# Attribute products of the edge MLP moved into the dense stage, stored sorted, and both gathers made to add to them

## What is computed

```
h = relu(layernorm(x))
x = x + rgcn(h)            # layer 0: two relational convolutions
h = relu(layernorm(x))
x = x + gcn(h)             # layer 1
h = relu(layernorm(x))
edge_feat = concat([h[src], h[dst], edge_attr])      # 512 + 512 + 64
messages = mish(mish(edge_feat @ W1 + b1) @ W2 + b2) # layer 2
agg = segment_sum(messages, dst)
u = mish(concat([h, agg]) @ W3 + b3)
x = x + layernorm(h + u @ W4 + b4) * gamma + beta
# layer 3: relu(concat(h[src], h[dst]) @ W.T + b), summed by src
```

## Time and profile before

| | |
|---|---|
| runs | 1164.44, 1168.77, 1169.74 us, median 1168.77 us |
| profiled execution | 1167.43 us, of which the span of the trace is 1165.6 us |
| busy in the span | PE 1082.5 us (93%), DVE 856.0 (73%), ACT 557.9 (48%), POOL 498.8 (43%) |

### The profile page before, as it was taken

How to read it: one execution, slowest core, us unless ns; L and a number is a source line. 1 busy time by engine, 2 the same in 40 slices (tenths; PEclk the granted TensorE clock), 3 DMA queues, 4 the chain that set the end, 5 groups by cost and what they waited for, 6 DMA issues and landing times. The chain is left out here.

```text
span 1165.6 us, 15308 instructions
## 1 busy us (share of the span) xinstructions
PE 1082.5 (93%) x4358; PEld 588.0 (50%) x4358; DVE 856.0 (73%) x2016; ACT 557.9 (48%) x978; POOL 498.8 (43%) x434
## 2 busy tenths in 40 slices
PE   3779888899999988999999999999999989999997
PEld 1133223344557453755555555555555547446664
DVE  5997667769755153787887887887887856848997
ACT  0221321311332311577777777777777734115564
POOL 0000112243333430768876666666666200027773
PEclk9788989999999999899999999999999999999999
DMA  7996997657111005685554444444444020026665
GB/s 281 366 361 229 362 379 272 229 186 248 63 50 46 13 14 193 143 251 112 115 105 99 97 96 99 96 97 98 97 97 76 2 74 3 9 84 202 210 211 160
DMA packets 60183, 172.65 MB, mean 148 GB/s; under 512 B 12646, under 2 KB 13190, under 8 KB 52553
## 3 DMA queue, kind: packets, MB, share of 16 engines
q0 software_dynamic: 31536, 72.01, 26.3%
q1 hardware_dynamic: 28568, 99.66, 23.2%
HBM read 159.65 MB, written 11.98 MB: 147 GB/s over the span
## 5 line engine op out<-in xcount | busy, mean ns | idle before, releaser
L1630 PE MATMUL PS<-wide,hidT 128*128 128x512 f32 x672 | 302.1, 592 | 0.0
L689 POOL DMA_INDIRECT rec_scratch<-rec_src,slot_row x84 | 99.0, 1179 | 262.5 <-DMA rec_scratch<-rec_src,slot_row 211.9
L1630 PEld LDWEIGHTS PS<-wide,hidT 128*128 128x128 f32 x672 | 128.6, 191 | 122.8 <-issue 120.5
L1566 ACT ACTIVATE wide<-PS 128x512 f32<-128x512 f32 x168 | 100.3, 597 | 100.5 <-PE PS L1616 64.2
L1453 POOL DMA_INDIRECT pair_sum<-table_j,counts_rec x84 | 136.1, 1620 | 27.6 <-issue 25.3
L1758 POOL DMA_INDIRECT u_space<-table_j,wide x87 | 83.0, 955 | 111.8 <-DMA table_j<-agg_space 84.9
L1445 POOL DMA_INDIRECT pair_sum<-table_i,counts_rec x84 | 89.3, 1063 | 97.1 <-PE PS L1616 59.7
L1571 ACT ACTIVATE wide<-wide,two 128x512 f32<-128x512 f32 x168 | 120.9, 719 | 6.2 <-DVE wide L1504 6.2
L1504 DVE SCALAR_TENSOR_TENSOR wide<-wide 128x512 f32<-128x512 f32 x168 | 116.3, 692 | 5.8
L1576 ACT ACTIVATE wide<-wide 128x512 f32<-128x512 f32 x168 | 105.8, 630 | 5.3
L1462 POOL DMA_INDIRECT rec_scratch<-rec_src,slot_row x84 | 87.5, 1041 | 41.1 <-issue 21.6
(11 more groups left out here) (321 smaller groups left out, 1849.2 us busy)
## 6 DMA issues: line engine op xcount, KB each, us to landing
pieces<-basis_rows SPq DMA_DIRECT2D x56, 1024.0 KB, 7.3
ring<-basis_low SPq DMA_DIRECT2D x30, 256.0 KB, 6.2
w_scratch<-pieces SPq DMA_DIRECT2D x112, 32.0 KB
counts_rec<-rec_scratch SPq DMA_DIRECT2D x1, 2856.0 KB, 9.5
rec_scratch<-rec_src,slot_row POOLq DMA_INDIRECT x168, 2.2
root<-L_gnn_root SPq DMA_DIRECT2D x2, 1024.0 KB, 6.2
rows_in<-in_rows_in SPq DMA_DIRECT2D x2, 1024.0 KB, 15.5
w_rel<-w_scratch SPq DMA_DIRECT2D x1, 2048.0 KB, 11.1
```

The source lines that it names most:

```text
L689: nc.gpsimd.indirect_dma_start(out=rec3_dram, out_offset=bass.IndirectOffsetOnAxis(ap=slot_row[:, 1, t:t + 1], axis=0), in_=rec, in_offset ...
L1566: nc.scalar.activation(grow[l][:, t % 2, :], PS[:, bank, :], ACT.Exp).then_inc(sem(f"exp{l}"), 1)
L1630: m = nc.tensor.matmul(o, hidT[:, t % 2, k * P:(k + 1) * P], w2[:, k, :], start=False, stop=(k == KT - 1), skip_group_check=True)
```

## The change

The attribute products no longer belong to the edge loop. In the dense stage the attributes come in already turned (`attr_T`, 21 slabs of 4 tiles, doubled over the partitions: the upper 64 rows hold the same values), loaded on ScalarE's queue. ScalarE rounds a slab to a short float (float32r), VectorE replaces the second 64 rows by the remainder, and the weights are split in two likewise. TensorE then makes 128 edges x 512 outputs in two short-float passes of 128x512 (`attr_rows`), ScalarE copies them out of PSUM (`keep_attr`), and GpSimd scatters the 2 KB rows to their sorted places in HBM (`scatter_attr`). The counts of products at each place are constants: 35 in `gathered_first`, 20 after the Y1 products, 15 in the root rows, 10 in `gathered`, 4 in `both`.

In the edge stage SyncE loads the finished rows of tile t into `pair_sum`, and both gathers add to them. `pre` is four transposes. The record that GpSimd sorts is now 8 bytes, and its 84 scatters run with three in flight, before the attribute scatters, and start without waiting for layer 3's records. `is_dst3` has six buffers instead of two. The last pair numbers are read ahead of the tail.

```diff
+REC = 2
+SLAB = 4
+SLABS = ET // SLAB
+        attr_dram = dram("attr_scratch", (P * ET, D))
+            ATTR_RING, REC_RING = 6, 3
+            attr_out = lambda t: slabs[:, 4 + t % ATTR_RING, :] if t % ATTR_RING < 4 else late_f[:, 7 * P + (t % ATTR_RING - 4) * D:7 * P + (t % ATTR_RING - 3) * D]
+            FIRST_ATTR = ((0, 0, 0, 2, 2), (2, 1, 2, 1, 1), (2, 1, 2, 1, 2), (2, 1, 2, 1, 2), (2, 1, 2, 1, 2))
+            Y1_ATTR, ROOT_ATTR, GATHER_ATTR, BOTH_ATTR = 2, 3, 2, 1
@@ TensorE, dense stage @@
+                def attr_rows(number):
+                    for _ in range(number):
+                        t = next(turned_attr)
+                        pe.wait_ge(sem("attr_lo"), t // SLAB + 1)
+                        bank = turn(("A", t), alone)
+                        own = attr_split[:, t // SLAB % 2, t % SLAB * P:(t % SLAB + 1) * P]
+                        nc.tensor.matmul(PS[:, bank, :], own, w_attr_hi[:], start=True, stop=False)
+                        nc.tensor.matmul(PS[:, bank, :], own, w_attr_lo[:], start=False, stop=True).then_inc(sem("side_mm"), 1)
@@ GpSimd, dense stage @@
-                def scatter(t, rec):
-                    if t:
-                        pool.wait_ge(sem("sorted1"), 16 * t)
+                def scatter(t):
+                    if t >= REC_RING:
+                        pool.wait_ge(sem(f"sorted1_{t % REC_RING}"), 16 * (t // REC_RING))
+                def scatter_attr(t):
+                    if t >= 3:
+                        pool.wait_ge(sem(f"attr_out{(t - 3) % ATTR_RING}"), 16 * ((t - 3) // ATTR_RING) + 16)
+                    pool.wait_ge(sem("side_ev"), side["A", t] + 1)
+                    nc.gpsimd.indirect_dma_start(
+                        out=attr_dram, out_offset=bass.IndirectOffsetOnAxis(ap=slot_row[:, 1, t:t + 1], axis=0),
+                        in_=attr_out(t), in_offset=None).then_inc(sem(f"attr_out{t % ATTR_RING}"), 16)
-                pool.wait_ge(sem("rec_set"), 2)
+                pool.wait_ge(sem("slot_row1"), 1)
+                for t in range(ET):
+                    scatter(t)
+                for t in range(ET):
+                    scatter_attr(t)
@@ VectorE, dense stage @@
+                def attr_low(j):
+                    dve.wait_ge(sem("attr_hi"), j + 1)
+                    low = attr_split[ED:P, j % 2, :]
+                    nc.vector.tensor_tensor(low, attr_in[ED:P, j % 2, :], low.bitcast(F32), ALU.subtract).then_inc(sem("attr_lo"), 1)
@@ ScalarE, dense stage @@
+                def keep_attr(number):
+                    for _ in range(number):
+                        t = next(kept_attr)
+                        j = t // SLAB
+                        if t >= ATTR_RING:
+                            act.wait_ge(sem(f"attr_out{t % ATTR_RING}"), 16 * (t // ATTR_RING))
+                        keep_product(("A", t), attr_out(t))
+                        if t % SLAB == 0 and j + 2 < SLABS:
+                            load_slab(j + 2)
+                        if t % SLAB == SLAB - 1 and j + 2 < SLABS:
+                            high_slab(j + 2)
-                for r in range(2):
-                    for m in range(NT):
+                for m in range(NT):
+                    keep_attr(ROOT_ATTR)
+                    for r in range(2):
                         act.wait_ge(sem("rests"), 2)
                         nc.scalar.copy(counts_short[r][:, m, :], counts[r][:, m, :]).then_inc(sem("counts_short"), 1)
@@ SyncE, edge stage @@
+                def load_attr(t):
+                    if t >= GOT3:
+                        sp.wait_ge(sem("pre_mm"), t - GOT3 + 1)
+                    sp.dma_start(pair_sum[:, t % GOT3, :], attr_tiles[:, t, :]).then_inc(sem(f"got3_a{t % GOT3}"), 16)
@@ GpSimd, edge stage: gather_i @@
-                    if t >= GOT3:
-                        pool.wait_ge(sem("pre_mm"), t - GOT3 + 1)
+                    pool.wait_ge(sem(f"got3_a{t % GOT3}"), 16 * (t // GOT3) + 16)
                     nc.gpsimd.indirect_dma_start(
                         out=pair_sum[:, t % GOT3, :], out_offset=None, in_=tables[0][0],
-                        in_offset=bass.IndirectOffsetOnAxis(ap=idx[:, t, 0:1], axis=0),
+                        in_offset=bass.IndirectOffsetOnAxis(ap=idx[:, t, 0:1], axis=0), compute_op=ALU.add,
@@ TensorE, edge stage: pre @@
-                    for k in range(KT):
-                        m = nc.tensor.matmul(PS[:, pre_bank(t), k * P:(k + 1) * P], w_attr[:, k * P:(k + 1) * P],
-                                             attr[:, t * P:(t + 1) * P], start=False, stop=True, skip_group_check=True)
```

More of the change, by code:

```diff
@@ L1317, in _, with load_slab, high_slab @@
                         keep_stage(piece(m), m)
-                for c in range(1, NT):
-                    keep_turned(("T1", c - 1), c - 1, True)
+                def load_slab(j):
+                    if j < 2:
+                        act.wait_ge(sem("side_mm"), side["Y0", 1, NT - 1] + 1)
+                    else:
+                        act.wait_ge(sem("attr_lo"), j - 1)
+                    nc.scalar.dma_start(attr_in[:, j % 2, :], a["attr_T"][j]).then_inc(sem(f"attr_in{j % 2}"), 16)
+                def high_slab(j):
+                    act.wait_ge(sem(f"attr_in{j % 2}"), 16 * (j // 2) + 16)
+                    if j >= 2:
+                        act.wait_ge(sem("side_mm"), side["A", SLAB * (j - 1) - 1] + 1)
+                    nc.scalar.copy(attr_split[:, j % 2, :], attr_in[:, j % 2, :]).then_inc(sem("attr_hi"), 1)
+                kept_attr = itertools.count()
+                def keep_attr(number):
[9 more added lines that the diff above has]
+                            high_slab(j + 2)
+                load_slab(0)
+                load_slab(1)
+                act.wait_ge(sem("w_attr_in"), 32)
+                nc.scalar.copy(w_attr_hi[:], w_attr[:]).then_inc(sem("w_attr_hi"), 1)
+                high_slab(0)
+                high_slab(1)
+                for c in range(NT):
+                    keep_attr(sum(FIRST_ATTR[c]))
+                    if c:
+                        keep_turned(("T1", c - 1), c - 1, True)
                 for c in range(NT):
@@ L1435, in _ @@
                 sp.dma_start(b3_col[:], a["in_b3_col"]).then_inc(sem("b3_in"), 16)
+                for t in range(GOT3, ET):
+                    load_attr(t)
             @block.gpsimd
@@ L1548, in _ @@
                         grown(0, s + 1)
-                    for j in late_turns:
-                        keep_turn(j)
                     if 0 <= s - 1 < ET:
@@ L1582, in high_part @@
                     nc.scalar.copy(mes_hi[:, t % KEPT3, :], mes[:, t % 2, :]).then_inc(sem("mes_hi"), 1)
-                for j in range(TURNS_ACT):
-                    act.wait_ge(sem("attr_tp"), j + 1)
-                    nc.scalar.copy(attr[:, j * D:(j + 1) * D], PS[:, j % NT, :]).then_inc(sem("attr_T"), 1)
                 for s in range(-1, ET + 1):
@@ L1692, in _ @@
                         pre(s + 1)
-                    for j in TURNS_AFTER.get(s, ()):
-                        turn(j)
                     if s == ET:
```

150 lines of the change are left out of this document (77 added, 73 removed).

## The result

The changed kernel is slower: median 1229.78 us (1227.50 to 1235.62, 4 runs) against 1167.97 us (1164.44 to 1169.74, 4 runs), ratio 1.0541, 95% interval [1.0493, 1.0589]. The profiled execution took 1227.50 us with a span of 1225.7 us, 60.1 us more than the span of before.

| part of the span | before | after | difference |
|---|---|---|---|
| up to the first gather | 240.88 | 236.25 | -4.6 |
| first gather to the end of the dense stage | 226.03 | 280.88 | +54.8 |
| edge stage | 487.02 | 499.84 | +12.8 |
| the rest | 211.67 | 208.73 | -2.9 |

A forecast was written before the change was run, and what follows sets the result against it. The prediction took TensorE to bound the dense stage and edge loop, with VectorE and ScalarE (5.15 us) and GpSimd next in the loop. 38.6 + 2 + 14 - 21 + 4.5 + 8 - 3 = +43 on 1167.4: 1210 us, range 1182 to 1243.

The forecast's parts named there:

- Dense products, +38.6: Dense stage: 168 short-float passes of 128x512 at 0.230 us add 38.6 us on a full TensorE, with nothing covering them.
- Casts, +2: Dense stage, before the second sum: one copy and two casts of the counts make TensorE wait 2 us (0 to 4).
- Stall in the first gather, +14: First gather: TensorE stops when GpSimd's scatters are late, slowed beside VectorE's weight sums; +14 us (0 to 35).
- The loop, -21: Edge loop: a tile falls from 5.46 us to about 5.2, over 82 tiles -21 us (-25 to -13).
- the ring of 5.15 us: Edge loop: VectorE and ScalarE in lockstep, each step waiting for the one before, need 5.15 us a tile.
- The start, +4.5: Start of the edge stage: first gather waits for a load, second DMA for an adding one; +4.5 us (0 to 8).
- Loads behind the weights, +8: Early edge loop: tile 9's load stands behind 4 MB of weights, so tile 6 is late; +8 us (0 to 20).
- The tail, -3: End of the edge stage: one-hots and numbers of the last pairs are ready, saving five waits of 0.57 us; -3 us.
- 1142 us (TensorE alone): Rival: both limits in the edge loop misread, it follows TensorE at 4.64 us a tile; 1142 us, chance 0.08.
- Two limits that beat: Rival: adding DMAs and loads raise latencies, so the edge loop gets no faster, 5.6 us a tile; 1243 us, chance 0.12.
- About no change: Rival: all stalls are nothing and the edge loop's ring is near 5.0 us; 1168 us, chance 0.05.
- the ring of one tile: Edge loop: the prediction's theory that VectorE and ScalarE set the period, 5.15 us a tile.

## Why the forecast held, and where it did not

The time lies in the range, and the direction is right, but 20 us of +62 were missed, and the terms were further off than their sum. In the profiled execution the edge stage was forecast at -21 + 4.5 + 8 - 3 = -11.5 us and came to +12.8, 24 us off; 7.5 us of that are hidden in the total by two parts that no term was about (-4.6 and -2.9 in the table).

1. *Dense products, +38.6.* Right as a size: passes start at 391.47, 391.70, 391.93 and 392.17 us, 0.233 apart, and 168 of them are 39.1 us. Incomplete as a reason: "Nothing covers it", but the second pass taken away gave 3.2 us instead of 19.6, since other limits lie just under it.
2. *Casts, +2.* Too small: 5.7 us of gap and 1.7 us of slower products, of which the moved pair gives 3 or more. The part left out is what comes after the wait: the gap ends 1.7 us after the last cast, and behind it the products run at a granted clock of 0.50.
3. *Stall in the first gather, +14.* Wrong in size: TensorE's waits there are 0.42, 0.63 and 0.53 us. The records were forecast to begin at 98 and end at 256 and did at 97.09 and 250.7. The slow DMAs of the earlier trace rows, 7.32 and 5.94 us, did not come back:

```profile
251.49 5.39 DVE L1035 SCALAR_TENSOR_TENSOR wide<-ring,att,wide 128x512 f32<-128x512 f32 x8
...
252.60 1.14 POOL L734 DMA_INDIRECT attr_scratch<-w_rel,slot_row  x1 [0.30 <-issue]
254.04 1.02 POOL L734 DMA_INDIRECT attr_scratch<-w_rel,slot_row  x1 [0.30 <-issue]
```

Scatters inside eight weight sums take 1.14 and 1.02 us. The Trainium skill (SBUF — State Buffer, Who interferes with whom) says that a VectorE instruction with two inputs in SBUF contends with a GpSimd instruction that reads SBUF. By this trace that costs little: the 19 attribute scatters that ran beside weight sums took 1.02 us in the median and 1.28 at most, the other 65 took 0.96 in the median, and the term's upper end fell. What made two scatters of before take 7.32 and 5.94 us stays open.

Terms 1 to 3 add up to 54.6 us, and the stage took 54.8 more. The sum is right by luck: 14 was too much, and the casts, a slow product at 322.70 (5.38 us instead of 3.70, with a granted clock of 0.50 from 324 to 327 us), and waits of 0.4 to 1 us took its place. The passes (39.1), the casts (7.4), that product (1.7) and five waits (3.0) make 51 us; the rest of the 54.8 is not traced to a cause.

4. *The loop, -21.* This is the step that failed. "VectorE splits the message from 891.61 ... That is 5.15 us round ... nothing in the ring that the change shortens": the ring of 5.15 us exists, and with the sum moved the loop runs at it, 5.08. But I closed it on the two engines and did not follow `mes_lo` to its reader. TensorE's sum stands in front of the message after the next, and so the longer ring goes over three engines and two tiles: 10.74 us against 2 x 5.46 = 10.92 before. Only 0.09 us a tile were to be won. The means 5.46 and 5.40 give 81 x 0.06 = 5 us instead of 21, and the period of 5.15 to 5.3 us that was to show the forecast right was not there. GpSimd was read rightly: `gather_i` takes 1.56 us (1.6 forecast), its iterations begin at 700.42, 705.54, 710.66 and 715.77 us, 5.12 a tile, and on average from 640 to 900 us they take 5.27, against 5.16 to 5.28.
5. *The start, +4.5.* 7.9 us, at the end of its bounds. I had counted one load ahead of the first gather; all nine are on the DMA engines, and the gather takes 8.25 us.
6. *Loads behind the weights, +8.* 12.3 us, shown by the run that moves them (-12.0, or 8 to 12). The mechanism was right. The load of tile 9 was back at 571.4, 20.9 us after the first weights were issued at 550.55; I had 14 to 27 and took 20. For 7.6 us of that SyncE was still issuing: the load of tile 9 was issued at 558.14. What I missed is that TensorE comes back slower, at a granted clock of 0.51: the second interval is 7.43.
7. *The tail, -3.* 2.8 us: from the last hidden tile to the next stage 19.23 before, 16.44 after.

Of the rivals, 1142 us (TensorE alone) fell with a loop of 5.40. "Two limits that beat" was near with its first words, the loop hardly gets faster, but not with its reason, for plain gathers leave the loop as it is, nor with its 5.6 us. "About no change" fell: the ring of one tile is near its 5.08 us, but it is not what the loop runs at.

## What to carry over

Before an engine is relieved, find what its work would wait for if it were empty, and follow each value to its last reader in the order of the instructions: a ring can close over several engines and several tiles, and its length is divided by the tiles that it holds. A cheap test is to leave the work out altogether; here it would have shown that all that the change takes off the loop is worth 9 us, against 39 us of new products. And where a loop sits 0.09 us above the next limit, two edits that are each worth nothing or 7 us are worth 31 us together.

## What the hardware showed beside this

- A short-float pass of 128 columns takes 0.111 us, one of 512 columns 0.233: four times the columns for twice the time.
- With nine loads of 256 KB issued ahead of it the first adding gather landed 8.25 us after its issue, with three ahead 5.15 us, and the third tile was no earlier. A plain gather took 7.55 us with nine ahead and 4.59 with none.
- TensorE's granted clock was 0.63 from 510 to 530 us in the changed kernel, where it was busy for 4.36 of 20 us, and 0.50 from 516 to 542, busy for 7.55 of 26; the first message, at 539.37, took 5.12 us instead of 3.60.
